# Two cross-attention layers on one core: keys kept in DRAM in stack order, two loads per stack, one unit earlier in layer 0, mask rows only at a change of batch

## The chip, the core and the metric

The kernel runs on one core of one Trainium2 chip. The time is device microseconds for one execution. Of the kernel before there are three timed runs, 1661.9, 1662.81 and 1664.44 us; the median is 1662.81 us. Every view of the profile comes from one profiled execution.

## The reference

Two cross-attention layers follow each other. x is (4, 256, 512), the context (4, 1601, 512), the mask (4, 1601). Both layers have 32 heads of 16 channels.

```
layer 0:  lin(x, W, A, B) = x @ W + 2 * (x @ A @ B)          A, B of rank 16
          q = lin(x), 32 heads; k, v = lin(context), 8 heads, each used by 4 query heads
          out = x + lin(softmax(q k^T / 4) v, Wo, Ao, Bo)
layer 1:  q = x @ Wq.T + bq; k, v = context @ W.T + b, 32 heads each
          scores where mask == 0 are -inf; softmax over the 1601 keys
          y = x + (softmax(q k^T / 4) v) @ Wo.T + bo
          out = (y - mean) / sqrt(var + 1e-5) * ln_g + ln_b
```

## The kernel before, in words

The work is cut into 64 **units** of four query heads: 32 in layer 0 (8 per batch, one key head each), 32 in layer 1 (8 per batch, four key heads each). For each unit TensorE makes, in this order but interleaved with other units' work:

- 32 **maximum matmuls** (ring, line 1057), 128 queries by 402 keys, in two halves of the partitions; VectorE reduces each to a chunk's maximum (line 1240). "collect" turns them into the negative row maxima of the unit, which SyncE writes to DRAM (`write m`, line 1561, 4 x 32 runs of 128 B) and loads as rows of the query stack (`load m`, line 1568);
- the **scores**, 13 key tiles (12 of 124 keys and one of 113) in two halves: 26 matmuls per unit in layer 0 (line 1070), 52 in layer 1 (line 1075). They need the unit's maxima. ScalarE takes their exponential (line 1154);
- the **values** (line 1093), 13 tiles of four matmuls.

Beside these run the **products**: keys (`k`, line 1001), values (`v`), queries (`q`, line 1046), output (`o`). A key product makes two chunks of 402 keys for 128 rows; a key sequence has two products, four chunks. There are 4 key sequences for layer 0 (one a batch; 8 units each) and 16 for layer 1 (2 units each), 80 chunks in all.

**The way of a key chunk.** ScalarE reads it from PSUM into `full` (two buffers, line 1165). GpSimd splits it into a rounded part and the rest, both in `k_parts` (two buffers, lines 1379 and 1381); it first waits until the chunk before last has landed in DRAM (`s_kdw`). SyncE writes both parts to `k_dram` (`write k`, line 1503), one DMA per chunk. Queries go the same way over `q_parts` and `q_dram`: `write q` (line 1513) is three DMAs per pair of units, each 4 x 32 runs of 1024 B, and `load q` (line 1523) one DMA per unit.

**The key stack.** Scores and maxima multiply stacked rows: per half of the partitions 16 rows of the rounded part, 16 of the rest, 16 fixed rows with the mask and ones (XROW), and 16 of the rounded part again. `k_stack` has three slots. Layer 0 has one stack per two units, layer 1 one per unit. `stack` (line 1546) is six DMAs of 16 partitions by two runs of 6404 B; in layer 1 two more (line 1552) bring the batch's mask row, each time.

**The order.** All engines follow one list of steps that `Plan` writes out in advance: it keeps a clock of each engine with fixed costs and picks the next piece of work. SyncE issues every DMA on one queue, in the order of that list, and waits at each step for its semaphores, so a step that waits holds up all behind it. `write_keys(now)` puts the pending writes (keys, queries, maxima) into the list, those that are due or, with None, all; `enter_unit(u)` at the start of unit u makes sure that the keys and queries of unit u + 2 are made, adds `load q` for it, and `load_stack` adds its stack. `s_scores` guards the reuse of a slot.

## Time and profile before

| | before |
|---|---|
| median of three timed runs | 1662.81 us |
| the profiled execution's own time | 1668.17 us |
| its span, first to last instruction | 1666.3 us |
| mean granted TensorE clock | 0.967 |
| TensorE matmuls busy | 1581.1 us, 95% |
| TensorE weight loads busy | 1133.7 us, 68% |
| VectorE busy | 1216.4 us, 73% |
| ScalarE busy | 1005.8 us, 60% |
| GpSimd busy | 177.6 us, 11% |
| moved by DMA | 168.22 MB in 93970 packets |

Busy is the time in which an engine works on an instruction; a wait is idle time put down to what ended it. The busy shares are means over the whole span: layer 0 is roughly the first 877 us, layer 1 the rest. "Issue" is idle time for which the profile shows no releaser. The share of DMA is the mean over the core's 16 DMA engines.

### The profile page before, as it was taken

What the parts mean: (1) busy time and instruction counts of PE and PEld (TensorE: products, weight loads), DVE (VectorE), ACT (ScalarE), POOL (GpSimd) and SP (SyncE); (2) the same over time, 40 slices, a digit from 0 to 9 for tenths busy, and PEclk for the clock granted to TensorE, in tenths of its full rate; (3) what the DMA queues carried; (4) which work ended last, traced back from release to release, by engine and by line L of the source; (5) the groups of instructions that cost most, each with busy time, mean ns of one, the idle gap of its engine ahead of it and who ended that gap; (6) DMA issues with size and microseconds to landing.
All of it is one profiled execution on the core that took longest, in us unless ns stands there. A gap on an engine that the chain in (4) does not pass through costs nothing.

```text
span 1666.3 us, 42831 instructions
## 1 busy us (share of the span) xinstructions
PE 1581.1 (95%) x17828; PEld 1133.7 (68%) x17828; DVE 1216.4 (73%) x2669; ACT 1005.8 (60%) x1855; POOL 177.6 (11%) x274
## 2 busy tenths in 40 slices
PE   6899999999999999899989999999989999999997
PEld 3657666676666765655667777776767677777763
DVE  2667778677777777678867777588777778778782
ACT  0146666566666666576656666656656666666665
POOL 2000221001221011121211110000000001000000
PEclk8789999999999999999999999999999999999998
DMA  8645542534454233455436455634375346644520
GB/s 218 140 130 143 123 109 81 145 75 93 103 141 122 63 78 84 82 118 138 101 81 124 89 94 90 156 58 81 71 149 85 65 69 123 128 76 71 85 40 14
DMA packets 93970, 168.22 MB, mean 101 GB/s; under 512 B 21900, under 2 KB 70060, under 8 KB 93776
## 3 DMA queue, kind: packets, MB, share of 16 engines
q1 hardware_dynamic: 93776, 165.48, 47.1%
q8 instruction: 140, 2.29, 0.7%
q14 instruction: 54, 0.44, 0.1%
HBM read 114.62 MB, written 48.78 MB: 98 GB/s over the span
## 4 chain that ended last, share of the span: by engine, by line
PE 87%; issue 5%; DMA 2%; DVE 2%; SPq 1%; ACT 1%; POOL 0%; DVEq 0%; POOLq 0%
PE value L1093 23%; PE ring L1057 14%; PE work L1001 13%; PE work L1021 13%; PE score L1070 9%; PE score L1075 7%; PE work L1046 4%; PE work L1115 3%; DVE chunk_max L1240 1%; PE work L1029 1%; DMA m_dram<-m_turned 1%; ACT p_sb L1154 1%; PE work L984 1%; DMA ctx_sb<-ctxT 0%; SPq L1431 0%
## 5 line engine op out<-in xcount | busy, mean ns | idle before, releaser
L1240 DVE TENSOR_REDUCE chunk_max<-ring 128x1 f32<-128x402 f32 x2048 | 1046.0, 567 | 314.1 <-PE ring L1057 304.7
L1154 ACT ACTIVATE p_sb<-score 124x512 f32<-124x512 f32 (+1 forms) x1664 | 929.8, 597 | 546.7 <-PE score L1070 278.8
L1057 PE MATMUL ring<-k_stack,q_stack 64*128 64x402 f32 x2048 | 728.7, 448 | 42.4 <-issue 32.9
L1057 PEld LDWEIGHTS ring<-k_stack,q_stack 64*128 64x128 f32 x2048 | 339.9, 189 | 143.4 <-issue 64.1
L1093 PE MATMUL value<-p_sb,v_sb 124*32 124x256 f32 x6656 | 432.1, 388 | 1.6 <-issue 0.8
L1070 PE MATMUL score<-q_stack,k_stack 64*124 64x512 f32 (+1 forms) x832 | 365.4, 506 | 5.1 <-ACT p_sb L1154 3.3
L1075 PE MATMUL score<-q_stack,k_stack 64*124 64x256 f32 (+1 forms) x1664 | 344.2, 315 | 4.1 <-ACT p_sb L1154 2.0
L1021 PE MATMUL work<-wv,ctx_sb 64*124 64x128 f32 x3840 | 333.4, 276 | 4.8 <-issue 4.7
L1021 PEld LDWEIGHTS work<-wv,ctx_sb 64*124 64x124 f32 x3840 | 317.8, 187 | 9.0 <-issue 6.2
L1001 PE MATMUL work<-ctx_sb,wk 64*128 64x402 f32 x1280 | 295.7, 507 | 2.2 <-ACT full L1165 1.0
L1093 PEld LDWEIGHTS value<-p_sb,v_sb 124*32 124x32 f32 x6656 | 184.5, 110 | 161.0 <-issue 51.9
L1075 PEld LDWEIGHTS score<-q_stack,k_stack 64*124 64x124 f32 (+1 forms) x1664 | 242.3, 184 | 58.1 <-ACT p_sb L1154 31.7
L1070 PEld LDWEIGHTS score<-q_stack,k_stack 64*124 64x124 f32 (+1 forms) x832 | 145.9, 185 | 94.9 <-ACT p_sb L1154 50.3
L1001 PEld LDWEIGHTS work<-ctx_sb,wk 64*128 64x128 f32 x1280 | 163.0, 188 | 20.2 <-issue 3.2
L1046 PE MATMUL work<-xt_sb,wq 64*128 64x128 f32 x1024 | 101.4, 294 | 1.1 <-DVE wq L1211 0.8
L1046 PEld LDWEIGHTS work<-xt_sb,wq 64*128 64x128 f32 x1024 | 92.6, 203 | 5.6 <-DVE wq L1211 2.4
L1379 POOL CAST k_parts<-full 128x402 fp32r<-128x402 f32 x80 | 41.4, 518 | 494.8 <-ACT full L1165 494.8
L1265 DVE STREAM_TRANSPOSE o_sb<-value 128x256 f32<-128x256 f32 x64 | 28.6, 448 | 69.4 <-PE value L1093 69.2
L1115 PE MATMUL work<-wo,att_t 64*128 64x512 f32 x256 | 76.2, 615 | 2.4 <-POOL att_t L1399 2.3
L1381 POOL TENSOR_TENSOR k_parts<-full,k_parts 128x402 fp32r<-128x402 f32 x80 | 77.3, 966 | 6.4
L1390 POOL CAST q_parts<-full 128x256 fp32r<-128x256 f32 x32 | 12.7, 398 | 604.6 <-DVE full L1233 347.1
L1176 ACT ACTIVATE v_sb<-work 124x512 f32<-124x512 f32 (+2 forms) x100 | 38.4, 451 | 62.9 <-PE work L1021 35.5
(64 smaller groups left out, 365.7 us busy)
## 6 DMA issues: line engine op xcount, KB each, us to landing
k_stack<-k_dram SPq DMA_DIRECT2D x288, 200.1 KB
k_dram<-k_parts SPq DMA_DIRECT2D x60, 402.0 KB, 3.2
ctx_sb<-ctxT SPq DMA_DIRECT2D x24, 992.0 KB, 12.2
q_stack<-q_dram SPq DMA_DIRECT2D x64, 256.0 KB, 3.7
q_dram<-q_parts SPq DMA_DIRECT2D x96, 128.0 KB
k_dram<-k_parts SPq DMA_DIRECT2D x20, 395.0 KB, 3.3
wq<-l_Wq SPq DMA_DIRECT2D x2, 1024.0 KB, 7.4
xt_sb<-xT SPq DMA_DIRECT2D x4, 512.0 KB, 11.6
```

The lines of the kernel that those rows point to most:

```text
L1001: done = engine.matmul(work[:, n, 0:MW], w[rows, k, col * P:(col + 1) * P], ctx_sb[rows, k, lo:lo + MW], start=(p == 0), stop=(p == 2 * KT ...
L1021: done = engine.matmul(work[0:TT, n, j * P:(j + 1) * P], ctx_sb[rows, k, t0:t0 + TT], w[rows, k, col * P:(col + 1) * P], start=(p == 0), s ...
L1046: done = engine.matmul(work[:, n, 0:P], wq[rows, k, col * P:(col + 1) * P], xt_sb[rows, z % 2, k, n * P:(n + 1) * P], start=(p == 0), stop ...
L1057: engine.matmul(ring[bank_of["max", u, half, m]][:, 0:MW], q_stack[rows, u % 3, j, q * P:(q + 1) * P], k_stack[rows, 2 * (z % 3) + (u % 2 ...
L1070: engine.matmul(score_bank[n % 2][0:tn, :], k_stack[rows, slot + u % 2, t0:t0 + tn], q_stack[rows, u % 3, :, :].rearrange("p j q -> p (j q)"),
L1075: done = engine.matmul(score_bank[n % 2][0:tn, j * S:(j + 1) * S], k_stack[rows, slot + j, t0:t0 + tn], q_stack[rows, u % 3, j, :], start= ...
L1093: done = engine.matmul(value_bank[32 * j:32 * j + 32, 0:S], v_sb[0:tn, seq % 2, i, head * VW:head * VW + 32], p_sb[0:tn, (2 * n + j % 2) % ...
L1115: done = engine.matmul(work[:, n, :], att_t[rows, z % 2, k, n * P:(n + 1) * P], wo[rows, k, :], start=(p == 0), stop=(p == 2 * KT - 1))
L1154: engine.activation(p_sb[0:tn, n % PLACES, :], score_bank[n % 2][0:tn, :], ACT.Exp, scale=SCALE).then_inc(s_exp, 1)
L1240: engine.tensor_reduce(chunk_max[:, u % 2, half, m // NM, m % NM:m % NM + 1], ring[bank_of["max", u, half, m]][:, 0:MW], AX.X, ALU.max)\
L1379: engine.tensor_copy(dst[:, 0, :], one).then_inc(s_part, 1)
L1381: engine.tensor_tensor(dst[:, 1, :], one, dst[:, 0, :], ALU.subtract).then_inc(s_part, 1)
```

## The change

`k_dram` gets the order of the stack: per key sequence four blocks, in each three parts of 32 rows (rounded, rest, rounded). A chunk is now written by three DMAs instead of one, one per part, and the rounded part twice. A stack is read by two DMAs, one per half, of 48 partitions with one run of 2 x 1601 numbers each. For this the fixed rows move behind the keys (XROW 48 instead of 32), the query rows follow them, and the columns of the key weights and biases are put in the order (row, pair) on the host. The mask rows are loaded only where the slot's last stack was of another batch or layer.

In the plan, an odd unit of layer 0 brings the stack of the unit after it too, one unit before it was asked for until now, and the key products of a batch are due one unit earlier. Pending writes are kept by kind: a stack or a key product flushes the key writes alone, `load q` the query writes; query writes are due three tiles after the product (one before), the maxima's write when the plan's VectorE is expected to be done, their load two tiles later. All else stays.

```diff
@@ -86,13 +86,25 @@
 
     def step(self, *name):
         if name[0] == "stack":
-            self.write_keys(None)
+            self.write_all("write k")
+        if name[0] == "load q":
+            self.write_all("write q")
         self.steps.append(name)
 
-    def write_keys(self, now):
-
-        while self.writes and (now is None or self.writes[0][0] <= now):
+    def write_later(self, after, *name):
+
+        self.writes.append((self.now + after, name))
+        self.writes.sort(key=lambda x: x[0])
+
+    def write_due(self, now):
+
+        while self.writes and self.writes[0][0] <= now:
             self.steps.append(self.writes.pop(0)[1])
+
+    def write_all(self, *kinds):
+
+        self.steps += [name for _, name in self.writes if name[0] in kinds]
+        self.writes = [x for x in self.writes if x[1][0] not in kinds]
 
 
 
@@ -132,14 +144,14 @@
             self.vector_free = max(self.vector_free, end) + (400 if kind == "q" else 1300)
             self.work_free = self.vector_free + self.HOP
         if kind == "k":
-            self.write_keys(None)
+            self.write_all("write k")
             for c in (2 * name[2], 2 * name[2] + 1):
                 self.key_number[name[1], c] = self.keys
                 self.split_number["k", name[1], c] = self.splits
                 self.keys += 1
                 self.splits += 1
                 self.step("read k", name[1], c)
-                self.writes.append((self.now + 3, ("write k", name[1], c)))
+                self.write_later(3, "write k", name[1], c)
         elif kind == "v":
             for n in range(len(self.readings(name[2]))):
                 self.step("read v", name[1], name[2], n)
@@ -147,7 +159,7 @@
             self.split_number[name] = self.splits
             self.splits += 1
             self.step("read q", name[1])
-            self.writes.append((self.now + 1, ("write q", name[1])))
+            self.write_later(3, "write q", name[1])
         else:
             z = name[1]
             for q in range(self.QT):
@@ -293,7 +305,9 @@
         if m == each - 1 and self.max_at[1 - half] >= self.max_at[half]:
             self.step("collect", unit)
             self.vector_free += 800
-            self.writes += [(self.now + 1, ("write m", unit)), (self.now + 2, ("load m", unit))]
+            late = 1 + int(max(0.0, self.vector_free - max(self.free)) / 1800)
+            self.write_later(late, "write m", unit)
+            self.write_later(late + 2, "load m", unit)
             self.rows_at[unit] = self.vector_free + self.LOAD_ROWS
             if self.next_stack == unit + 2:
                 self.load_stack()
@@ -362,7 +376,6 @@
         self.product("q", 0)
         self.fold("v")
         self.step("read mask")
-        self.write_keys(None)
         self.load_queries(0)
         self.load_queries(1)
         self.step("load rest")
@@ -382,7 +395,7 @@
         self.budget = 16000.0
         for b in range(1, B):
             start = UB * (b - 1) * NT
-            todo += [(start + (UB - 2) * NT - 5, start + 2, ("k", b, g)) for g in k]
+            todo += [(start + (UB - 3) * NT - 5, start + 2, ("k", b, g)) for g in k]
             todo += [(start + UB * NT - 2, start + 2, ("v", b, g)) for g in v]
             end = start + UB * NT if b < B - 1 else (L0 - 4) * NT
             todo += [(end, start + 2, ("k", B + 4 * b + j, g)) for j in range(4) for g in k]
@@ -515,8 +528,10 @@
         if u + 2 < self.UNITS:
             for g in range(self.NM // 2):
                 self.ensure("k", self.seq_of(u + 2), g)
+            if u % 2 and u + 3 < L0:
+                for g in range(self.NM // 2):
+                    self.ensure("k", self.seq_of(u + 3), g)
             self.ensure("q", (u + 2) // 2)
-            self.write_keys(None)
             self.load_queries(u + 2)
             self.next_stack = u + 2
             if u in self.rows_at:
@@ -537,10 +552,16 @@
     def load_stack(self):
 
         u = self.next_stack
-        self.step("stack", u)
-        if u >= self.L0 or u % 2 == 0:
-            self.arrival = max(self.arrival, max(self.free) + 2000) + self.LOAD_STACK
-        self.stack_at[u] = self.arrival
+        early = (u + 1,) if u % 2 and u + 1 < self.L0 else ()
+        for n in (u,) + early:
+            if n in self.stack_at:
+                continue
+            if n >= self.L0 or n % 2 == 0:
+                self.step("stack", n)
+                self.arrival = max(self.arrival, max(self.free) + 2000) + self.LOAD_STACK
+                self.stack_at[n] = self.arrival
+            else:
+                self.stack_at[n] = self.stack_at[n - 1]
         self.stacked, self.next_stack = u, None
         self.load_ctx()
 
@@ -561,7 +582,7 @@
         self.exp_end[s, half] = self.scalar_free + self.AFTER
         self.score_free[n % 2] = self.exp_end[s, half] + self.HOP
         self.budget += self.plan_rate() / 2
-        self.write_keys(s)
+        self.write_due(s)
         if self.next_stack is None and s % self.NT < 6:
             self.load_ctx()
 
@@ -724,7 +745,7 @@
         self.s, self.half = s, half
 
     def end(self):
-        self.write_keys(None)
+        self.write_all("write k", "write q", "write m", "load m")
         z = 2 * self.B - 1
         while self.turns:
             self.turn(min(self.turns))
@@ -768,9 +789,9 @@
     CHUNKS = ROWS * NM
 
 
-    KPARTS = ((0, 0), (1, 1), (3, 0))
-    QPARTS = ((0, 0), (1, 0), (3, 1))
-    XROW = 2 * HD
+    KPARTS = ((0, 0), (1, 1), (2, 0))
+    QPARTS = ((0, 0), (1, 0), (2, 1))
+    XROW = 3 * HD
     VW = HD + 1
     VCOLS = 8 * VW + 15
     NEG = -1.0e30
@@ -811,8 +832,13 @@
 
 
     def source(z):
-        return (z // 4, z % 4 * 2 * HD, 2 * HD) if z < L0 // 2 else \
-            (B + (z - L0 // 2) // 2, z % 2 * 4 * HD, 4 * HD)
+        return (z // 4, z % 4) if z < L0 // 2 else (B + (z - L0 // 2) // 2, z % 2 * 2)
+
+    def batch_of(z):
+        return (z - L0 // 2) // UB if z >= L0 // 2 else None
+
+    def mask_changes(z):
+        return z >= L0 // 2 and batch_of(z) != batch_of(z - 3)
 
     def max_window(c):
         return min(c * MW, T - MW)
@@ -848,7 +874,7 @@
         att_t = sb("att_t", [P, 2, KT, S])
         row_bias = sb("row_bias", [P, 3, H])
         col_bias = sb("col_bias", [P, 3, KT])
-        k_dram = nc.dram_tensor("k_dram", [5 * B, 2, P, T], F32R, kind="Internal").ap()
+        k_dram = nc.dram_tensor("k_dram", [5 * B, 4, 3, 2 * HD, T], F32R, kind="Internal").ap()
         q_dram = nc.dram_tensor("q_dram", [4, 2, 4, HD, 2 * S], F32R, kind="Internal").ap()
         ident = sb("ident", [P, P])
         valid = sb("valid", [TT, B, NT])
@@ -914,7 +940,7 @@
 
         kst_loads, total = [], [0, 0, 0]
         for z in range(stack_of(UNITS - 1) + 1):
-            total[z % 3] += 6 + 2 * (z >= L0 // 2)
+            total[z % 3] += 2 + 2 * mask_changes(z)
             kst_loads.append(16 * total[z % 3])
 
         split_done = {name: 2 * (n + 1) for name, n in plan.split_number.items()}
@@ -1375,7 +1401,7 @@
                     dst = k_parts[:, n % 2, :, 0:hi - lo]
                     e.wait_ge(s_taken["k"], n + 1)
                     if n >= 2:
-                        e.wait_ge(s_kdw[n % 2], 16 * (n // 2))
+                        e.wait_ge(s_kdw[n % 2], 16 * len(KPARTS) * (n // 2))
                     engine.tensor_copy(dst[:, 0, :], one).then_inc(s_part, 1)
                     e.wait_ge(s_part, parts + 1)
                     engine.tensor_tensor(dst[:, 1, :], one, dst[:, 0, :], ALU.subtract).then_inc(s_part, 1)
@@ -1463,7 +1489,7 @@
             e.wait_ge(s_x_rows, X_ROWS)
             load_x_rows(0)
             e.wait_ge(s_q_rows, Q_ROWS)
-            engine.dma_start(raw(q_dram[:, :, 2, :, :]).rearrange("u h d n -> d (u h) n"),
+            engine.dma_start(raw(q_dram[:, :, 3, :, :]).rearrange("u h d n -> d (u h) n"),
                              q_rows.rearrange("d (o n) -> d o n", o=1).broadcast_to([HD, 8, 2 * S])).then_inc(s_qx, 16)
             engine.dma_start(wv0[:, :, :], by_tile(w0["Wv"])).then_inc(s_w["wv0"], 16)
             rows = 0
@@ -1500,8 +1526,9 @@
                     seq, c = a
                     (at, lo, hi), n = keys_of(c), plan.key_number[seq, c]
                     e.wait_ge(s_part, split_done["k", seq, c])
-                    engine.dma_start(raw(k_dram[seq, :, :, lo:hi]).rearrange("a p t -> p a t"),
-                                     raw(k_parts[:, n % 2, :, 0:hi - lo])).then_inc(s_kdw[n % 2], 16)
+                    for r, part in KPARTS:
+                        engine.dma_start(raw(k_dram[seq, :, r, :, lo:hi]), raw(k_parts[:, n % 2, part, 0:hi - lo]))\
+                            .then_inc(s_kdw[n % 2], 16)
                 elif kind == "write q":
                     pair, = a
                     first = 2 * pair % 4
@@ -1528,24 +1555,21 @@
                     z = stack_of(u)
                     if u < L0 and u % 2:
                         continue
-                    (seq, row, count), g = source(z), z % 3
+                    (seq, block), g = source(z), z % 3
                     for c in range(NM):
                         n = plan.key_number[seq, c]
-                        e.wait_ge(s_kdw[n % 2], 16 * (n // 2 + 1))
+                        e.wait_ge(s_kdw[n % 2], 16 * len(KPARTS) * (n // 2 + 1))
                     if z >= 3:
                         e.wait_ge(s_scores, 2 * NT * (last_of_stack(z - 3) + 1))
                     else:
                         e.wait_ge(s_kx[g], 32)
-                    for r, part in KPARTS:
-                        keys = raw(k_dram[seq, part, row:row + count, :])
-                        for half in range(2):
-
-                            own = keys.rearrange("(j d) t -> d j t", j=2) if u < L0 else \
-                                keys.rearrange("(j e d) t -> e d j t", j=2, e=2)[half]
-                            at = 64 * half + HD * r
-                            engine.dma_start(raw(k_stack[at:at + HD, 2 * g:2 * g + 2, :]), own).then_inc(s_kst[g], 16)
-                    if u >= L0:
-                        b = (u - L0) // UB
+                    for half in range(2):
+                        keys = k_dram[seq, block + (half if u >= L0 else 0)].rearrange("r (d j) t -> (r d) (j t)", j=2)
+                        engine.dma_start(
+                            raw(k_stack[64 * half:64 * half + XROW, 2 * g:2 * g + 2, :]).rearrange("p a t -> p (a t)"),
+                            raw(keys)).then_inc(s_kst[g], 16)
+                    if mask_changes(z):
+                        b = batch_of(z)
                         e.wait_ge(s_mask, 1)
                         for half in range(2):
                             at = 64 * half + XROW
@@ -1574,7 +1598,7 @@
                     e.wait_ge(s_out_row, rows)
                     engine.dma_start(out[b, q * P:(q + 1) * P, :], x_sb[:, b * QT + q, :]).then_inc(s_out, 16)
             for s, sem_k in enumerate(s_kdw):
-                e.wait_ge(sem_k, 16 * (plan.keys // 2))
+                e.wait_ge(sem_k, 16 * len(KPARTS) * (plan.keys // 2))
             e.wait_ge(s_out, 16 * rows)
 
         block = ctx.enter_context(nc.Block())
@@ -1603,7 +1627,13 @@
         arrays[f"l0_A{n}T"] = a[f"L0_xattn_A{n}"].T
         arrays[f"l0_B{n}"] = a[f"L0_xattn_B{n}"]
         arrays[f"l1_W{n}"] = a[f"L1_xattn_W{n}"].T
-    arrays["l1_bk"] = a["L1_xattn_bk"].reshape(H // 128, 128).T
+
+    order = np.arange(128).reshape(4, 2, 16).transpose(0, 2, 1).reshape(128)
+    for n in ("l0_Wk", "l0_Bk"):
+        arrays[n] = arrays[n][:, order]
+    order = np.arange(H).reshape(H // 64, 2, 2, 16).transpose(0, 2, 3, 1).reshape(H)
+    arrays["l1_Wk"] = arrays["l1_Wk"][:, order]
+    arrays["l1_bk"] = a["L1_xattn_bk"][order].reshape(H // 128, 128).T
 
     order = np.arange(H).reshape(H // 64, 2, 2, 16).transpose(0, 2, 3, 1).reshape(H)
     for n in ("l0_Wq", "l0_Bq", "l1_Wq"):
```

## Rows read from the trace of the kernel before

**Rows 1.** Waits: engine, line, releaser; us in total, times, longest

```profile
PE ring L1057 <- issue: 32.9, 11, 5.8
PE ring L1057 <- DMA q_stack<-q_dram: 2.8, 1, 2.8
PE score L1075 <- DMA q_stack<-m_dram: 1.8, 2, 1.3
PE score L1070 <- DMA q_stack<-m_dram: 1.3, 1, 1.3
```

**Rows 2.** Timeline, SyncE and TensorE, three gaps: start us, duration us, instruction

```profile
230.29 0.38 SPq L1503 DMA_DIRECT2D k_dram<-k_parts  x1
233.24 2.75 SPq L1546 DMA_DIRECT2D k_stack<-k_dram  x6
...
246.08 0.42 PE L1057 MATMUL ring<-k_stack,q_stack 64*128 64x402 f32 x1 [2.35 <-issue]
...
680.37 2.75 SPq L1546 DMA_DIRECT2D k_stack<-k_dram  x6
...
692.88 0.67 PE L1057 MATMUL ring<-k_stack,q_stack 64*128 64x402 f32 x1 [5.81 <-issue]
...
847.92 2.89 SPq L1546 DMA_DIRECT2D k_stack<-k_dram  x6
...
863.23 0.70 PE L1057 MATMUL ring<-k_stack,q_stack 64*128 64x402 f32 x2 [4.99 <-issue]
```

**Rows 3.** Stretches: length, busy by engine, granted clock, DMA share, GB/s; then nine summed

```profile
243.70:246.10 2.40, 0.05 (x3) 0.05 (x2) 0.80 (x5) 1.56 (x3) 1.59 (x3) 1.00 0.22 27
246.80:250.20 3.40, 3.40 (x32) 2.31 (x26) 0.98 (x3) 0.63 (x2) 0.69 (x1) 0.51 0.61 222
690.60:697.40 6.80, 4.52 (x33) 4.40 (x35) 2.09 (x4) 1.59 (x3) 0.00 (x0) 0.50 0.49 130
...
sum 40.90, PE 34.69 PEld 29.56 DVE 16.18 ACT 11.18 POOL 0.69; mean PE 3.85 PEld 3.28 DVE 1.80 ACT 1.24 POOL 0.08
```

**Rows 4.** SyncE's DMA issues: count, ns least/median/most, first to last start in us

```profile
L1546 SPq DMA_DIRECT2D k_stack<-k_dram x288: 310/423/2036, 32.4 to 1592.5; - x144
L1552 SPq DMA_DIRECT2D k_stack<-neg_row x64: 558/600/688, 824.8 to 1593.6; - x64
L1503 SPq DMA_DIRECT2D k_dram<-k_parts x80: 359/382/2697, 22.0 to 961.2; - x80
L1513 SPq DMA_DIRECT2D q_dram<-q_parts x96: 503/522/1275, 39.4 to 1554.8; - x96
```

**Rows 5.** Stretches of one transfer each: stack load, key write, query write

```profile
235.50:243.00 7.50, 7.50 (x81) 5.16 (x78) 5.44 (x12) 4.21 (x8) 0.00 (x0) 1.00 1.08 132
131.00:132.50 1.50, 1.50 (x24) 1.04 (x21) 0.22 (x1) 0.40 (x1) 0.00 (x0) 1.00 0.79 281
319.50:321.50 2.00, 2.00 (x17) 1.34 (x15) 1.96 (x4) 1.68 (x3) 0.00 (x0) 1.00 0.27 88
```

**Rows 6.** Timeline of SyncE: writes of keys and queries, and the maxima behind them

```profile
95.01 2.05 SPq L1513 DMA_DIRECT2D q_dram<-q_parts  x3
97.11 0.53 SPq L1561 DMA_DIRECT2D m_dram<-m_turned  x1
102.33 0.58 SPq L1568 DMA_DIRECT2D q_stack<-m_dram  x2
...
189.99 1.80 SPq L1503 DMA_DIRECT2D k_dram<-k_parts  x2
...
202.44 2.00 SPq L1503 DMA_DIRECT2D k_dram<-k_parts  x2
...
218.59 1.95 SPq L1503 DMA_DIRECT2D k_dram<-k_parts  x2
220.66 0.52 SPq L1561 DMA_DIRECT2D m_dram<-m_turned  x1
222.98 0.54 SPq L1568 DMA_DIRECT2D q_stack<-m_dram  x2
...
420.12 1.94 SPq L1503 DMA_DIRECT2D k_dram<-k_parts  x2
...
614.54 1.94 SPq L1503 DMA_DIRECT2D k_dram<-k_parts  x2
...
890.32 1.83 SPq L1503 DMA_DIRECT2D k_dram<-k_parts  x2
```

**Rows 7.** Timeline of TensorE: first scores of units 6, 14, 22 and 33

```profile
230.26 0.49 PE L1070 MATMUL score<-q_stack,k_stack 64*124 64x512 f32 x1
...
429.92 0.39 PE L1070 MATMUL score<-q_stack,k_stack 64*124 64x512 f32 x1
...
626.21 0.49 PE L1070 MATMUL score<-q_stack,k_stack 64*124 64x512 f32 x1
...
901.43 0.28 PE L1075 MATMUL score<-q_stack,k_stack 64*124 64x256 f32 x1
```

## The prediction

> **What bounds the kernel now.** I read the busy shares first, then who waits for whom, then the stretches around the longest gaps. TensorE is busy 1581.1 of 1666.3 us, in every slice but the first nine tenths or more, so a microsecond counts only if TensorE stands, or runs slowly, because of it. In the table of waits its largest idle group is the maximum matmul (ring, line 1057) with 32.9 us in 11 times, put down to "issue", that is, to nothing the profile could name; the matmuls that wait for DMAs of the row maxima are small [rows 1]. The name is found by setting the queue beside the gap. At 233.24 us SyncE issues the six loads of stack 8, 2.75 us of issuing; the next maximum, which needs that stack, starts at 246.08 after 2.35 us of nothing [rows 2]. The same stands before the two longest gaps: 12.5 us from the first issue (680.37) to the matmul at 692.88, 15.3 us (847.92) to that at 863.23 [rows 2]. So the 32.9 us are waits for key stacks.
>
> A gap costs more than itself. TensorE's granted clock is 1.00 before it, which is 2.4 GHz, and 0.50 (1.2 GHz) for 3.4 or 6.8 us from about its end [rows 3]. Nine such stretches sum to 34.69 us of busy TensorE; half of that, some 17 us, is lost. What perfect stacks could return is 32.9 + 17 = 50 us.
>
> **The loads.** Six DMAs of 200 KB become two of 600 KB, and the mask DMAs (64) stay only where batch_of(z) differs from batch_of(z - 3), three a batch, 12 stacks, 24 DMAs. From the medians [rows 4] a stack takes 6 x 0.42 = 2.5 us of SyncE now and 0.9 us after, plus 1.2 us less for the mask in 20 of 32 units of layer 1. A stack moves 1.23 MB: in the middle of such a load the queue's share is full (1.08) at only 132 GB/s [rows 5], so 9.3 us. The shapes change, 48 partitions with 12.8 KB in a row instead of 16 partitions with twice 6.4 KB. Bounds: 9.3 us at the row's rate, 4.4 us at the 281 GB/s which the key write reaches. I take 6.5 us, between them. A stack then lands about 1.6 + 3 = 4 to 5 us earlier in all of layer 0 and 5 to 6 in layer 1, which covers each gap but those at 687 (5.8 us) and 858 (5.0 us); in layer 0 it is also asked for one unit, about 25 us, earlier, which covers the one at 687. Other waits for the vector engine stand behind these, so I count 42 of the 50 us as gain.
>
> The Trainium skill, "SBUF — State Buffer", section "Door 1: The DMA port swizzle", has it that a transfer's rate depends on how many of 16 ports its partitions reach: 16 partitions reach 4 ports (about 109 GB/s), 48 in a row reach 8. The row's 132 GB/s at a full share is near that; by the rule a half stack needs 8 x 12.8 KB / 27.2 GB/s = 3.8 us and the stack at most 7.6 us, an estimate by that page, which would leave the gain the same.
>
> **The writes of keys, the other side.** A chunk's write is one DMA now, with 128 partitions outermost (128 x 2 runs of 1608 B). It becomes three, and with the order block (4), part (3), row (32) the destination is 4 blocks of 32 rows. The kernel has one transfer of exactly this form: the query write (line 1513), 4 by 32 runs of 1024 B. In a stretch where only such writes run, the DMA share is 0.27 and the rate 88 GB/s; where key writes run it is 0.79 and 281 GB/s [rows 5]. So four outermost rows keep a quarter of the 16 DMA engines busy, each at full speed. I expect the key write to fall from 16 engines to 4.
>
> Its size: a third is 128 x 1608 B = 206 KB, at 88 GB/s 2.3 us; a chunk 7 us, a pair of chunks (they are always written in pairs) 14 us, instead of 823 KB at 281 GB/s = 2.9 us. There are 80 chunks from 22 to 961 us [rows 4], in layer 0 often every 12 to 16 us [rows 6]. Over 40 pairs four engines get 560 us of work. Every transfer that follows needs these four or some of them: the stacks and the queries are spread over all engines, the maxima (line 1561) have the 4 by 32 form themselves. Bounds for a pair: 2.9 x 3/2 = 4.4 us if the new form ran as wide as the old, 14 us by the query write. I take 14, since the form is equal.
>
> The Trainium skill, "DMA: Bandwidth & Descriptors", section "Why a DMA increments its semaphore by 16 and not by 1", says that a DMA is split over the largest number up to 16 that divides the slowest dimension of both sides. For 128 against 4 by 32 that is 4, for the stack's 48 it is 16; the rows of the query write agree, and by it the three key writes stay on the same four engines.
>
> **What that makes late.** The scores of a unit wait for its row maxima, which go to DRAM and back. How a narrow write delays them is in the trace: after three query writes at 95.01 us the maxima are written at 97.11 and their load is issued only at 102.33, 5.2 us later; without anything ahead it is 2.3 us (220.66 to 222.98), also just behind a pair of key writes as they are now [rows 6]. With 14 us in the queue I get first score no earlier than key write + 18 us (1.3 us to start, 14, and about 3 for write, load and landing). Unit 6: 218.59 + 18 = 236.6 against 230.26, late by 6.3 us. Unit 14: 420.12 + 18 against 429.92, 8.2 us. Unit 22: 614.54 + 18 against 626.21, 6.3. Unit 33: 890.32 + 18 against 901.43, 6.9 [rows 6, 7]. Done for all 64 units from the same view: 21 are late, all from 5 to 35, together some 85 us. No cover is at hand: TensorE works its stream in order, and what stands behind the score (values, maxima of the next unit) waits with it.
>
> The loads of queries and of stacks 33 to 36 are issued at a unit's start, often straight behind a pair, as at 230.29 [rows 2]: I give them 30 us, between 0 (where the next maximum is 15 us away, as in unit 6) and 60. The k_parts buffers are freed by the landing of the write: pairs only 12 us apart (190.0, 202.4) then hold GpSimd's split and, one pair later, ScalarE's read of the product, with the exponentials behind it in ScalarE's queue; 15 us, bounds 0 and 50. SyncE gains and loses about equally: 192 + 40 DMAs fewer, 160 more of 0.5 us, all beside TensorE.
>
> The late arrivals are gaps of 2 to 8 us, each followed by half clock as above, 1.7 to 3.4 us lost. For 16 to 20 of them: 35 us. Moving the writes in the planner (query write three tiles after its product, the maxima's load two tiles after their write) lets key writes pass ahead of the maxima, never the reverse; cost 0 to 20, taken as 0, since 21 units are counted already. Padding and order of weight columns change no instruction: 0.
>
> **Sum**, against the profiled execution (1668.2 us, span 1666.3): -42 + 85 + 30 + 15 + 35 = +123, so 1791. The three timed runs have their median 5.4 us lower; I forecast 1786, about 7.5% slower.
>
> **Rivals.** (a) *Wide writes.* The new key write is spread over 16 engines after all, or its queue is drained before anyone asks. Then only the gain is left: 1663 - 42 = 1621, or 1640 if the maxima are still now and then late. For it: stacks are clearly what TensorE waits for. Against it: the quarter share of the query write. It decides where a pair takes under 7 us: then the maxima's 5 us of slack and the planner's room hold. 0.17. (b) *Narrow, but mostly absorbed.* The plan is made anew, the key products fall elsewhere, late units catch up since VectorE (73%) and ScalarE (60%) have room: half of the 85, 15 for the rest, 15 for the clock: 1663 - 42 + 72 = 1693. 0.22. (c) *Backlog on backlog.* Ten pairs per batch of 200 us are 140 us, with the query writes, contexts and stacks the four engines come to over 90%, and one delay pushes the next: double the m, query and clock terms, 1663 - 42 + 230 = 1850 and more. 0.15. (d) *The gain and the loss cancel* at 1663, within 0.2% (3.3 us, what a measurement can tell from no change): 0.04. The forecast's own case, 1730 to 1830: 0.42.
>
> Range: from 1650, which takes in the upper part of (a), to 1870. Faster 0.17, same 0.04, slower 0.79.
>
> **What would show it.** Right: in a stretch of layer 0 with key writes alone the DMA share is near 0.25 and the rate near 90 GB/s; from the maxima's write to the issue of their load there are over 10 us behind a pair; TensorE's idle time before the score matmuls (under 5 us now for DMAs) grows to tens of us; the 11 gaps before maxima are mostly gone, and layer 1 beyond 1000 us is a few us shorter than its 666 us. Wrong: share 0.8 in key writes, or the maxima's load within 3 us of their write; then the time goes below 1650.

## The result, and the profile after

The changed kernel takes 1889.04 us (median of four runs, 1884.84 to 1892.64) against 1663.62 us for the one before in the same runs: ratio 1.1345, 95% interval 1.1305 to 1.1385. It is 13.5% slower. The direction was forecast, and so was the four-engine write behind it; the size was not: 1786 us, in a range that ended at 1870.

The profiled execution has a span of 1890.9 us, 224.6 us more. TensorE's waits after (engine, line, what ended them; us, times, longest), to set beside [rows 1]:

```profile
PE score L1096 <- DMA q_stack<-m_dram: 118.0, 21, 13.9
PE ring L1083 <- DMA q_stack<-q_dram: 53.2, 10, 21.6
PE score L1101 <- DMA q_stack<-m_dram: 24.1, 5, 8.9
PE ring L1083 <- DMA k_stack<-neg_row: 20.6, 2, 10.4
```

The 32.9 us of nameless waits for stacks are gone. In their place stand 142 us of scores that wait for their maxima, 53 for queries and 21 for stacks (the mask row is a stack's last DMA). Busy time of each engine, then:

```profile
PE 1633.4 (86%) x17828; PEld 1162.7 (61%) x17828; DVE 1223.1 (65%) x2669; ACT 1009.0 (53%) x1855; POOL 180.1 (10%) x274
```

TensorE stands idle for 257.5 us instead of 85.2, 172.3 more, and the same 17828 matmuls take 52.3 us more: that is the half clock after gaps (mean granted clock 0.91 against 0.967; half of TensorE's busy time at a granted clock of 0.50 is 99 us, 44 before). The two make up the 224.6 us. Where it happens, by stretch (length, busy of TensorE, weight loads, VectorE, ScalarE, GpSimd, granted clock, DMA share, GB/s):

```profile
0.00:100.00 100.00, 58.28 (x403) 40.55 (x403) 37.87 (x75) 5.00 (x10) 10.57 (x22) 0.75 0.63 162
...
300.00:500.00 200.00, 166.55 (x1654) 115.70 (x1656) 124.41 (x271) 105.34 (x192) 25.79 (x37) 0.91 0.36 100
...
900.00:1100.00 200.00, 158.89 (x1496) 111.82 (x1490) 112.23 (x235) 93.48 (x172) 24.75 (x35) 0.88 0.38 102
...
1300.00:1500.00 200.00, 196.99 (x2619) 149.26 (x2617) 161.93 (x367) 127.72 (x241) 11.45 (x20) 1.00 0.47 95
```

The loss ends with the last key write: from there (1190.8 us) to the end it is 700.1 us, before from 961.2 us 705.2. And the write itself, in stretches with key writes alone, then a stack load; they answer to [rows 5], 281 and 132 GB/s:

```profile
300.00:312.00 12.00, 11.93 (x129) 9.33 (x129) 8.91 (x21) 7.66 (x14) 2.31 (x3) 1.00 0.27 92
544.50:546.50 2.00, 2.00 (x31) 1.60 (x24) 1.29 (x4) 1.62 (x4) 0.63 (x1) 1.00 0.27 89
...
1258.30:1266.30 8.00, 7.31 (x72) 4.27 (x68) 7.41 (x17) 5.17 (x10) 0.61 (x1) 1.00 0.99 149
```

A quarter of the DMA engines, 92 GB/s, as the query write had it. The stack load gained little, 149 GB/s against 132. What it does to one unit, on SyncE's queue and then TensorE (start us, duration us); it answers to [rows 6, 7], where the load of the maxima is issued 2.3 us after their write:

```profile
157.89 7.42 SPq L1530 DMA_DIRECT2D k_dram<-k_parts  x6
165.44 1.83 SPq L1585 DMA_DIRECT2D m_dram<-m_turned  x1
175.60 0.54 SPq L1592 DMA_DIRECT2D q_stack<-m_dram  x2
...
177.17 0.76 PE L1096 MATMUL score<-q_stack,k_stack 64*124 64x512 f32 x1 [9.41 <-DMA q_stack<-m_dram]
```

From the first key write to the first score are 19.3 us; the forecast had put 18. Of the 64 loads of maxima 20 are issued more than 10 us after the maxima's write; before there is none. One more thing has changed, SyncE's own time for issuing a key write (count, ns least/median/most, first to last start in us; before in [rows 4]):

```profile
L1530 SPq DMA_DIRECT2D k_dram<-k_parts x240: 502/944/5453, 22.1 to 1190.8; - x120
```

All issues of key writes take 284 us of SyncE, 35 before. In the chain of work that ended last DMAs and SyncE's issuing (SPq) have grown from 3% to 38% of the span (first line before, second after):

```profile
PE 87%; issue 5%; DMA 2%; DVE 2%; SPq 1%; ACT 1%; POOL 0%; DVEq 0%; POOLq 0%
PE 53%; DMA 26%; SPq 12%; issue 4%; POOL 2%; DVE 1%; ACT 1%; POOLq 0%; DVEq 0%; ACTq 0%
```

### The profile page after: what moved, and what is told of

It reads as the page before. It is cut to its first block, busy times and chain, and to the rows that moved or that the text cites. A ratio compares the mean times of both kernels' runs of the same rounds, so it can differ in the third digit from the quotient of the medians.

```text
span 1890.9 us, 42759 instructions
## 1 busy us (share of the span) xinstructions
PE 1633.4 (86%) x17828; PEld 1162.7 (61%) x17828; DVE 1223.1 (65%) x2669; ACT 1009.0 (53%) x1855; POOL 180.1 (10%) x274
## 4 chain that ended last, share of the span: by engine, by line
PE 53%; DMA 26%; SPq 12%; issue 4%; POOL 2%; DVE 1%; ACT 1%; POOLq 0%; DVEq 0%; ACTq 0%
PE value L1119 14%; DMA m_dram<-m_turned 11%; PE work L1047 9%; SPq L1530 9%; DMA k_dram<-k_parts 9%; PE ring L1083 9%; PE score L1101 6%; PE work L1027 5%; PE score L1096 4%; DMA q_stack<-m_dram 4%; PE work L1072 2%; PE work L1141 2%; DMA q_dram<-q_parts 1%; POOL k_parts L1407 1%; PE work L1055 1%
## 5 line engine op out<-in xcount | busy, mean ns | idle before, releaser
L1083 PE MATMUL ring<-k_stack,q_stack 64*128 64x402 f32 x2048 | 743.0, 456 | 77.9 <-DMA q_stack<-q_dram 53.2
L1096 PE MATMUL score<-q_stack,k_stack 64*124 64x512 f32 (+1 forms) x832 | 393.2, 539 | 120.5 <-DMA q_stack<-m_dram 118.0
L1119 PE MATMUL value<-p_sb,v_sb 124*32 124x256 f32 x6656 | 452.2, 400 | 2.1 <-ACT p_sb L1180 1.2
L1083 PEld LDWEIGHTS ring<-k_stack,q_stack 64*128 64x128 f32 x2048 | 345.9, 194 | 170.4 <-issue 101.1
L1101 PE MATMUL score<-q_stack,k_stack 64*124 64x256 f32 (+1 forms) x1664 | 338.4, 319 | 27.8 <-DMA q_stack<-m_dram 24.1
L1027 PE MATMUL work<-ctx_sb,wk 64*128 64x402 f32 x1280 | 313.9, 539 | 2.0 <-ACT full L1191 1.0
L1101 PEld LDWEIGHTS score<-q_stack,k_stack 64*124 64x124 f32 (+1 forms) x1664 | 238.9, 186 | 89.8 <-issue 37.3
L1096 PEld LDWEIGHTS score<-q_stack,k_stack 64*124 64x124 f32 (+1 forms) x832 | 153.3, 194 | 216.1 <-issue 98.2
L1027 PEld LDWEIGHTS work<-ctx_sb,wk 64*128 64x128 f32 x1280 | 174.3, 202 | 26.9 <-issue 7.6
L1072 PE MATMUL work<-xt_sb,wq 64*128 64x128 f32 x1024 | 96.8, 292 | 1.0 <-DVE wq L1237 0.8
```

The costliest lines, as they stand in the source:

```text
L1027: done = engine.matmul(work[:, n, 0:MW], w[rows, k, col * P:(col + 1) * P], ctx_sb[rows, k, lo:lo + MW], start=(p == 0), stop=(p == 2 * KT ...
L1072: done = engine.matmul(work[:, n, 0:P], wq[rows, k, col * P:(col + 1) * P], xt_sb[rows, z % 2, k, n * P:(n + 1) * P], start=(p == 0), stop ...
L1083: engine.matmul(ring[bank_of["max", u, half, m]][:, 0:MW], q_stack[rows, u % 3, j, q * P:(q + 1) * P], k_stack[rows, 2 * (z % 3) + (u % 2 ...
L1096: engine.matmul(score_bank[n % 2][0:tn, :], k_stack[rows, slot + u % 2, t0:t0 + tn], q_stack[rows, u % 3, :, :].rearrange("p j q -> p (j q)"),
L1101: done = engine.matmul(score_bank[n % 2][0:tn, j * S:(j + 1) * S], k_stack[rows, slot + j, t0:t0 + tn], q_stack[rows, u % 3, j, :], start= ...
L1119: done = engine.matmul(value_bank[32 * j:32 * j + 32, 0:S], v_sb[0:tn, seq % 2, i, head * VW:head * VW + 32], p_sb[0:tn, (2 * n + j % 2) % ...
```

## The experiments

Ratios are to the kernel before, timed beside each. The diffs show only the lines that matter, shortened.

**1. The write alone** (plan, stack loads, mask rows of before):

```diff
-k_dram = [5 * B, 2, P, T];  k_dram[seq, :, :, lo:hi] <- k_parts[:, n % 2, :, 0:hi - lo]
+k_dram = [5 * B, 4, 3, 2 * HD, T]
+for r in range(3): k_dram[seq, :, r, :, lo:hi] <- k_parts[:, n % 2, KPARTS[r][1], 0:hi - lo]
```

> The kernel before, its plan and its six loads per stack unchanged; only the write of a key chunk is the change's: three DMAs of 4 blocks x 32 rows. Theory N (the narrow writes are the loss): 1850 to 1950 us, since the stall of the stacks (32.9 us) stays and is joined by maxima and queries that arrive late; a pair of chunks keeps four DMA engines busy for 14 us. Rival P (the new order of writes in the plan is what makes maxima and queries late, the writes themselves hide): under 1720 us.

Measured: 1956.72 us, ratio 1.1761 (1.1729 to 1.1793), just above the range given. The write alone costs more than the whole change: 291 us. The rest of the change gives 68 us of it back. The likely reason is that the stacks are late here too (63.2 + 27.8 us, against 20.6 in the changed kernel):

```profile
PE score L1072 <- DMA q_stack<-m_dram: 64.5, 16, 12.1
PE ring L1059 <- DMA k_stack<-k_dram: 63.2, 7, 13.1
PE ring L1059 <- DMA q_stack<-q_dram: 47.2, 5, 22.6
PE ring L1059 <- DMA k_stack<-neg_row: 27.8, 2, 16.0
```

**2. The plan alone** (class Plan of the changed kernel in the kernel before, nothing else):

```diff
-class Plan: as before
+class Plan: as changed
```

> The kernel before with the change's plan alone (layer 0's stacks one unit earlier, key products due earlier, query writes three tiles late, the maxima's write and load by expected time); writes and loads of keys as before, one wide DMA a chunk. Theory N: no slower than before, 1635 to 1670 us, the early stacks taking back up to 30 us in layer 0. Rival P: 1720 us or more, with waits of score matmuls for the maxima of tens of us.

Measured: 1664.12 us, ratio 1.0001 (0.9983 to 1.0019): no difference. The waits say that two effects cancel:

```profile
PE score L1091 <- DMA q_stack<-m_dram: 19.5, 2, 17.7
PE score L1096 <- DMA q_stack<-m_dram: 14.6, 4, 11.6
PE ring L1078 <- issue: 9.3, 4, 3.2
```

The nameless stack waits fall from 32.9 to 9.3 us, but two gaps of 17.7 and 11.6 us open before scores. The second one on SyncE and TensorE:

```profile
1546.98 0.52 SPq L1582 DMA_DIRECT2D m_dram<-m_turned  x1
1551.41 0.33 SPq L1544 DMA_DIRECT2D q_stack<-q_dram  x1
1551.80 2.76 SPq L1567 DMA_DIRECT2D k_stack<-k_dram  x6
1554.60 1.29 SPq L1573 DMA_DIRECT2D k_stack<-neg_row  x2
1555.94 0.82 SPq L1589 DMA_DIRECT2D q_stack<-m_dram  x2
...
1565.34 0.57 PE L1096 MATMUL score<-q_stack,k_stack 64*124 64x256 f32 x1 [11.63 <-DMA q_stack<-m_dram]
```

The maxima's load, two tiles "late" in the plan, comes to stand behind a query load and a stack of 1.2 MB. The other gap is unit 0, whose maxima stand behind four context loads of 1 MB: its first score starts at 91.9 us, before at 77.4. From there the early stacks gain: the first score of unit 28 comes 19 us earlier than before. The gaps further on take that back (both are single executions).

**3. The changed kernel with the plan of before:**

```diff
-class Plan: as changed
+class Plan: as before
```

> The changed kernel with the plan of before: three narrow writes, two loads per stack, mask rows only at a change of batch, but the order of steps of before. Theory N: within 3% of the changed kernel, 1840 to 1920 us. Rival P: near before, under 1720 us. If it lies well between, both count.

Measured: 1871.0 us, ratio 1.124 (1.1205 to 1.1274). The order has at most a small part in the loss: without the new plan the kernel is 18 us faster and still 12.4% slower than before. Nearly all of the 18 us lies at the start, where the first score of unit 0 comes at 94.3 us instead of 110.0.

**4. The same rows, written wide:**

```diff
-k_dram = [5 * B, 4, 3, 2 * HD, T];  k_dram[seq, :, r, :, lo:hi]
+k_dram = [5 * B, 4, HD, 3, 2, T];   k_dram[seq, :, :, r, :, lo:hi] as "b d j t -> (b d) j t"
-stack: k_dram[seq, block] as "r (d j) t -> (r d) (j t)"
+stack: k_dram[seq, block] as "d r j t -> (d r) (j t)"
+query load: per half 48 rows "r d n -> d r n" and 16 fixed rows, four DMAs instead of one
```

> The changed kernel with the key layout in DRAM turned to [block][row][part][pair], so that the 128 rows of a chunk are at one distance and each of the three writes has 64 rows of 2 runs outermost instead of 4 blocks; a stack is still two loads of 48 partitions with 12.8 KB in a row. The query load becomes four DMAs per unit to match the row order; query writes stay as they were. Theory N: 1610 to 1670 us, at or below before, DMA share near 0.8 or more in key writes. Rival B (three writes and half again as many bytes are the cost, however wide): above 1720 us. Rival P: above 1720 us as well, but with the waits at the maxima.

Measured: 1652.49 us, ratio 0.9923 (0.9898 to 0.9947). All 225 us are back and 11 more, with the same three writes, the same bytes and the same plan. The query load had to change with the layout, from one DMA to four. A stretch of key writes alone:

```profile
502.50:504.50 2.00, 2.00 (x29) 1.15 (x18) 1.07 (x4) 0.62 (x2) 0.00 (x0) 1.00 1.07 362
```

**5. Three wide writes in the kernel before** (the third part written too, 128 rows at one distance), the control for experiment 1:

```diff
-k_dram = [5 * B, 2, P, T], one write a chunk
+k_dram = [5 * B, 3, P, T]; for r in range(3): k_dram[seq, r, :, lo:hi] <- k_parts[:, n % 2, KPARTS[r][1], ...]
```

> The kernel before, plan and six loads per stack unchanged, but a chunk is written by three DMAs with 128 rows outermost (the third part written too): as many DMAs and bytes as in e1_narrow_only, only wide. Theory N: 1660 to 1680 us, at most 1% over before; e1_narrow_only then owes all but this to four outermost rows. Rival B (three issues and 823 KB more of writes a pair are the cost): over 1750 us.

Measured: 1666.14 us, ratio 1.0026 (1.0002 to 1.0049). Three issues and half again the bytes cost 0 to 0.5%. SyncE's issues, as many as in the changed kernel, are short here (112 us in all):

```profile
L1506 SPq DMA_DIRECT2D k_dram<-k_parts x240: 319/446/3271, 22.1 to 967.9; - x120
```

**6. Two narrow writes a chunk** (experiment 1 without the third part; the stack reads the first part twice):

```diff
-for r in range(3): k_dram[seq, :, r, :, lo:hi] <- ...
+for r in range(2): k_dram[seq, :, r, :, lo:hi] <- ...
```

> Two narrow writes a chunk instead of three, 4 blocks x 32 rows, plan and stack loads of before: a pair keeps four engines for 9.4 us instead of 14. If each microsecond of queue costs the same (linear), two thirds of e1_narrow_only's loss: 1665 + 0.67 x 291 = 1860 us. If there is a threshold (5 us of slack before the scores, pairs 12 to 16 us apart, and delay feeding on delay above it), far less: 1730 to 1790 us.

Measured: 1787.49 us, ratio 1.0775 (1.0736 to 1.0813). Two thirds of the queue time, 42% of the loss.

**7. Eight rows outermost** instead of four, else as experiment 1:

```diff
-k_dram = [5 * B, 4, 3, 2 * HD, T]
+k_dram = [5 * B, 8, 3, HD, T]
```

> As e1_narrow_only (three writes a chunk, plan and stack loads of before), but DRAM in 8 blocks of 16 rows, so eight rows outermost. If the number of engines is the outermost count: DMA share near 0.5 in key writes, a pair takes 7 us, which is near the 5 us of slack of the maxima: 1670 to 1710 us. If instead any write that isn't in one piece is spread badly: near e1_narrow_only, over 1850 us.

Measured: 1743.7 us, ratio 1.0462 (1.0429 to 1.0494). The count of engines came as forecast, half of them:

```profile
550.50:552.50 2.00, 0.60 (x8) 0.18 (x1) 1.43 (x4) 0.00 (x0) 0.00 (x0) 1.00 0.53 179
```

The time did not: I had said 1670 to 1710. The maxima mostly keep their slack (scores wait 16.3 us for them), but the stacks, late already before, are later:

```profile
PE ring L1059 <- issue: 73.2, 19, 8.6
PE ring L1059 <- DMA q_stack<-q_dram: 13.3, 2, 13.1
```

Experiments 5, 7, 6 and 1 share plan and loads, so they make a curve, though bytes and number of engines differ too: a pair occupies its engines for 3.5, 7, 9.3 and 14 us (from the rates 357, 179 and 89 GB/s and the bytes), the cost is 2, 78, 124 and 291 us. Up to 9.3 us each microsecond of a pair costs some 20 us, above it 36. A threshold at the slack of 5 us, as experiment 6 had weighed it, does not show: at 7 us 78 us are lost already.

**8. The changed kernel with the maxima first:** pending writes and loads of the maxima go ahead of a query load and of a context load.

```diff
+        if name[0] in ("load q", "load ctx"):
+            self.write_all("write m", "load m")
```

> The changed kernel, narrow writes and all, whose plan puts pending writes and loads of the maxima ahead of a query load and of a context load. With wide writes this was worth 17 us. If order adds to width: 1865 to 1875 us. If the queue of key writes hides it (the maxima wait for the four engines either way): within 0.5% of 1889 us.

Measured: 1869.5 us, ratio 1.1243 (1.1203 to 1.1282): 20 us better than the changed kernel. The order adds to the width.

**9. Wide writes with the plan of before:**

```diff
-class Plan: as changed, with the layout of experiment 4
+class Plan: as before, with the layout of experiment 4
```

> Wide key writes and two loads per stack as in e3_wide, but the plan of before. It tells what layout and loads are worth alone. Theory: the stacks land in about 11 us instead of 13 to 15, which fills about half of the 32.9 us at the maxima: 1640 to 1655 us. Rival (a stack load of 48 partitions is no faster, 8.4 us against 9.3, and only the early request helps): 1655 to 1668 us, with 20 us or more still idle before maximum matmuls.

Measured: 1665.65 us, ratio 1.0002 (0.9979 to 1.0025). The theory was wrong and the rival right: layout, two loads and fewer mask rows bring nothing by themselves, and the wait they were to shorten is still there:

```profile
PE ring L1063 <- issue: 31.0, 10, 6.1
```

It is the early request that takes these waits away (9.3 us are left in experiment 2, 1.9 in experiment 4). But the plan alone brings nothing either; only both together make the 13 us of experiment 4. Unit by unit, in one execution each, the layout adds 1.5 us to the plan's time at unit 28 and has taken 18 us off it at unit 63, so it pays in layer 1. Part of its price here is the query load of four DMAs: one gap of 8.2 us at the start waits for it.

**10. Query writes wide too**, experiment 4's plan:

```diff
-q_dram = [4, 2, 3, HD, 2 * S];  write as "u h d (j s) -> (u h) (d j) s"
+q_dram = [4, 2, HD, 3, 2 * S];  write as "u h d (j s) -> (u h d) j s"
-query load: 48 rows "r d n -> d r n"
+query load: 48 rows "d r n -> (d r) n", one piece
```

> e3_wide with the query writes wide too (rows at one distance, 64 by 2 runs outermost). Theory N says that four-row writes cost where something waits behind them: the maxima behind a query write (5 us late now) come 3 us earlier, one of the two gaps at the maxima in e3_wide (10.6 us, unit 60) shrinks: 1640 to 1652 us. Rival: query writes are too small to matter, same as e3_wide within 0.3%.

Measured: 1635.14 us, ratio 0.983 (0.9791 to 0.9869): 17 us better than experiment 4. How much of it is the write is not shown, since the query load is in one piece now too and SyncE issues it faster (76.9 us in all, now 53.7). And it isn't where I said: the gap at unit 60 is unchanged (10.3 us). Unit by unit, in one execution each, the gain comes in three places: 6.6 us before the first score, then 5.5 and 5.7 us between units 44 and 56, where two gaps of about 2 us are gone and the half clock after them with them.

**11. Experiment 4 with the maxima first** (diff of experiment 8):

> e3_wide whose plan puts pending writes and loads of the maxima ahead of a query load and of a context load. The two gaps of 18.9 us (unit 0, behind four context loads of 1 MB) and 10.6 us (unit 60, behind a query load and a stack) should go, with the half clock behind them: 1652 - 30 - 5 = 1617 us, range 1610 to 1635. Rival: the plan made anew puts them elsewhere, or the maxima's order makes stacks late again: 1640 to 1660 us.

Measured: 1635.48 us, ratio 0.9817 (0.9781 to 0.9852). The gap at unit 60 is gone, the one at unit 0 fell only from 18.9 to 12.0 us, so 17 us instead of 35, just outside the range given.

**12. All of it** (experiments 4, 10 and 8):

> e8_wide_maxima_first with wide query writes. If both hold: 1610 to 1630 us, at or up to 5 us below e8_wide_maxima_first. Rival: no further gain, since no wait is left behind a query write.

Measured: 1614.5 us, ratio 0.9698 (0.9664 to 0.9732), 3.0% faster than the kernel before and the best of all. It is within the range, but 21 us below experiment 11, not the 5 us at most that I had said. TensorE is idle for 53 us of 1617.8:

```profile
PE 1564.8 (97%) x17828; PEld 1120.6 (69%) x17828; DVE 1216.3 (75%) x2669; ACT 1006.0 (62%) x1855; POOL 178.2 (11%) x274
```

## Why the prediction was right and wrong, by its steps

**Four engines: right.** It was read off the query write [rows 5], a transfer of the same form, and holds for the key write (share 0.27, 89 to 92 GB/s). With 8 rows outermost the share is 0.53, with 64 it is 1.07. The rule of the Trainium skill cited for it ("DMA: Bandwidth & Descriptors", "Why a DMA increments its semaphore by 16 and not by 1") agrees at all three counts. It was wrong that a pair under 7 us would hide: with 8 rows a pair takes 6.9 us and costs 78 us (experiment 7).

**A pair takes 14 us, first score at key write + 18 us: right** (617 KB x 2 / 89 GB/s = 13.9 us; 19.3 us in the unit shown).

**The sum over it: wrong, and this is the step that failed.** Maxima 85 us were 142; query and stack loads 30 were 74 (53.2 + 20.6); the half clock 35 was 52 net of what the vanished gaps gave back. SyncE's issues, which I had put at nothing ("gains and loses about equally"), grew by 221 us in all (433 to 654), since a narrow key write takes 1.2 us to issue on average and a wide one 0.5 (experiment 5), and they stand in the chain. I had added up delays pair by pair on the old timetable and had given the k_parts buffers 15 us. In the runs the delays pile up: the first score is 33 us late at unit 0, 58 at unit 7, 109 at unit 16, 206 at unit 32, 227 at unit 36, and no more after that. The chain of work that ended last shows what ran instead, in layer 0 from 225 us (start us, us, what):

```profile
228.32 12.74 DMA k_dram<-k_parts
241.78 0.89 POOL k_parts L1407
243.83 11.29 DMA k_dram<-k_parts
255.84 0.90 POOL k_parts L1407
257.59 8.31 DMA k_dram<-k_parts
...
270.91 11.16 DMA m_dram<-m_turned
```

Here it is a loop: write, landing, GpSimd's split into the freed buffer, next write. Of the chain from 225 to 370 us 47% is key writes, 19% SyncE's issuing of them, 16% the maxima behind them, and TensorE's own work some 6%. GpSimd waits for the buffers 230.8 us in 32 times (never named in the waits of before):

```profile
POOL k_parts L1405 <- DMA k_dram<-k_parts: 230.8, 32, 18.7
```

It waits 150.0 us in experiment 1, 34.0 with two narrow writes and 10.2 with eight rows. In this stretch the maxima's write is issued straight behind six key writes again and again (245.3, 303.4, 347.2 us), and in layer 0 late units are the rule (21 score waits there, 5 in layer 1).

That the delays feed on each other fits the curve, whose last part is the steepest. By what way they do is only argued. The buffer loop is one way; another is SyncE's long issues, a third the queue of the four engines alone, which also holds the maxima (11% of the whole chain is their write). Against the loop as the main cause stands experiment 3: GpSimd waits only 110.9 us there, and nearly as much time is lost. No run had a third k_parts buffer or a second queue for the key writes, which would tell.

The time came near rival (c), backlog on backlog, at 1850 and more, to which I had given 0.15. Its sum does not fit its own words: doubling the maxima, query and clock terms gives 300 us, with 15 for the buffers 1936 us, and not 1850. So its number came near by luck, its mechanism not. It deserved more weight for the reason that it names, that one delay pushes the next: slack read off the old timetable did not hold here.

**The start was left out.** The first score of unit 0 starts at 109.98 us, 77.4 before: 33 us late, with a gap of 21.6 us before the first maximum and 13.9 us before the first score. Two things add up. The narrow writes with the plan of before make it 17 us (experiment 3; SyncE issues the first twelve key writes for 20 us), the new plan alone 14.5 us (experiment 2), since the maxima stand behind context loads.

**The gain of 42 us: near in size, wrong in reason.** In experiment 4 the nameless waits are 31 us shorter and TensorE's busy time 10 us, though new gaps at the maxima take most of it back. The waits did not go since a stack load is quicker: it takes 8.3 us, not 6.5 (1.23 MB at 149 GB/s; bounds 4.4 and 9.3), and with the plan of before nothing is gained (experiment 9). The early request took 24 us of waits away (experiment 2). The port rule of the Trainium skill cited for it ("SBUF — State Buffer", "Door 1: The DMA port swizzle") gave at most 7.6 us for a stack, nearer than my 6.5, and still below the measured one.

**"The planner's moves cost 0": wrong**, and my reason, that key writes passing ahead of the maxima was already counted, missed what else passes ahead: context loads, query loads and stacks. 17 to 20 us in experiments 8 and 11, about 30 us of gaps in experiment 2, 18 us between experiment 3 and the changed kernel.

**The three issues and more bytes at nothing: right for wide writes alone**, 0 to 0.5% (experiment 5); for narrow ones see SyncE's issues above.

## What to carry to other kernels

Look at the outermost dimension of both sides of every DMA that a layout change touches: the key write fell here from 128 rows at one distance to 4 blocks of rows, kept 4 of 16 DMA engines, and what stood behind it in the queue paid. If such a form exists in the old trace, the share and rate of a stretch with it alone are the price. And when the new load on one resource comes near the time at hand, do not add delays one by one on the old timetable: look for what then sets the pace (here the queue of four engines, the issues of SyncE and a double buffer freed by the write all stood in the chain), and forecast from that.

## What the runs showed that was not expected

- A load of 48 partitions with 12.8 KB in a row is hardly faster than three of 16 with 6.4 KB: 149 against 132 GB/s at a full share of all engines, while writes in runs of 1.6 KB reach 281 to 362 GB/s.
- The engines that a narrow write leaves free do move what is queued behind it: just behind the pair issued at 139.9 us a stack load follows, and from 147.5 to 157 us the share is 0.87 and the rate 232 GB/s. Late is what needs the four: the maxima's write, of the 4 by 32 form itself, makes 11% of the chain. With eight engines the write alone still costs 4.6%.
- Making the 96 narrow query writes wide, and their loads one piece, gave some 17 us in a kernel of 1650 (experiments 4 and 10), a third of it at the start.
